# Top-k weights by halves, a later square root and fewer fillers in one expert layer, diagonal blocks on GpSimd in another

## The reference

```python
h = _rmsnorm(x, norm_w)
scores = jax.nn.softmax(flat @ router_w.T, axis=-1)
topk_w, topk_ids = lax.top_k(scores, K)                  # K = 4
topk_w = topk_w / jnp.sum(topk_w, axis=-1, keepdims=True)
act = jax.nn.silu(g) * u                                  # per chosen expert
routed = jnp.sum(y.reshape(T, K, H) * topk_w[..., None], axis=1)
shared = jax.nn.silu(flat @ sg) * (flat @ su) @ sd
out = residual + (routed + shared).reshape(B, S, H)
```

```python
scores = jax.nn.sigmoid((xf @ gate_w.T).astype(jnp.float32))
_, sel = jax.lax.top_k(scores + expert_bias, TOP_K)      # TOP_K = 2
xq = mxfp8_qdq(routed * ts_sorted[:, None])
h = jax.nn.silu(h1) * h3
routed_out = jax.lax.ragged_dot(mxfp8_qdq(h), w2q, counts)
```

## Time and profile before

| what | us |
|---|---|
| median of 3 runs | 1478.41 |
| lowest and highest | 1473.91, 1485.47 |
| the profiled execution | 1473.91 |
| its span | 1472.2 |
| mean granted clock of TensorE | 0.944 of full speed |

### The profile page before, as it was taken

How to read it: one execution, slowest core, us unless ns; L and a number is a source line. 1 busy time by engine, 2 the same in 40 slices (tenths; PEclk the granted TensorE clock), 3 DMA queues, 4 the chain that set the end, 5 groups by cost and what they waited for, 6 DMA issues and landing times. The chain is left out here.

```text
span 1472.2 us, 25588 instructions
## 1 busy us (share of the span) xinstructions
PE 1236.5 (84%) x9839; PEld 846.4 (57%) x9839; DVE 1145.4 (78%) x2253; ACT 872.1 (59%) x1155; POOL 296.9 (20%) x231
## 2 busy tenths in 40 slices
PE   3899998564887988877889999978896999998687
PEld 1577776442334555556656766745683766766454
DVE  5788786498888999929578999956896899897553
ACT  3677766522666787813166666734893667665453
POOL 0000000100141111000005155240460165155000
PEclk9999999877998999978999999999999999999889
DMA  6699989102005999983269998950554999989500
GB/s 240 118 182 178 198 164 177 57 1 90 11 1 105 185 200 196 192 188 66 97 109 196 184 186 166 167 148 22 173 172 135 167 171 173 173 153 167 108 1 8
DMA packets 561641, 199.55 MB, mean 136 GB/s; under 512 B 547200, under 2 KB 547584, under 8 KB 560256
## 3 DMA queue, kind: packets, MB, share of 16 engines
q1 hardware_dynamic: 561536, 198.15, 66.7%
HBM read 60.48 MB, written 0.26 MB: 41 GB/s over the span
## 5 line engine op out<-in xcount | busy, mean ns | idle before, releaser
L596 DVE SCALAR_TENSOR_TENSOR arena<-L_xattn_sm,L_xattn_rr,arena 128x1024 f16<-128x1024 f32 x192 | 274.9, 1472 | 11.2 <-ACT arena L495 10.9
L570 DVE CUSTOM_DVE_ANT_0 L_xattn_sm<-ps,L_xattn_bias 128x1024 f32<-128x1024 f32 x192 | 231.0, 1221 | 59.6 <-issue 56.6
L495 ACT ACTIVATE arena<-L_xattn_sm,L_xattn_rr 128x1024 f16<-128x1024 f32 x192 | 210.1, 1141 | 112.2 <-DVE L_xattn_rr L587 111.3
L399 PE MATMUL ps<-ctxT,L_xattn_qk 128*128 128x512 f16 x1152 | 267.1, 382 | 6.9 <-DVE L_xattn_qk L557 6.5
L485 ACT ACTIVATE L_xattn_sm<-L_xattn_sm,L_xattn_nm 128x2048 f32<-128x2048 f32 x96 | 192.2, 2002 | 77.0 <-DVE L_xattn_nm L579 76.1
L411 PE MATMUL ps<-arena,ctx 128*128 128x128 f16 x3072 | 194.9, 224 | 29.1 <-DMA arena<-arena 28.9
L411 PEld LDWEIGHTS ps<-arena,ctx 128*128 128x128 f16 x3072 | 182.7, 100 | 44.4 <-DMA arena<-arena 33.2
L399 PEld LDWEIGHTS ps<-ctxT,L_xattn_qk 128*128 128x128 f16 x1152 | 111.8, 99 | 135.9 <-DVE L_xattn_qk L557 9.0
L421 PEld LDWEIGHTS ps<-arena,ctx 128*128 128x128 f16 x1536 | 94.1, 98 | 22.8 <-DMA arena<-arena 5.4
L421 PE MATMUL ps<-arena,ctx 128*128 128x128 f16 x1536 | 102.2, 220 | 3.8 <-DMA arena<-arena 3.7
L2114 PE MATMUL ps<-arena 128*128 128x512 f16 x384 | 91.8, 391 | 0.0
(11 more groups left out here) (527 smaller groups left out, 2071.4 us busy)
## 6 DMA issues: line engine op xcount, KB each, us to landing
arena<-in_L_xattn_w SPq DMA_DIRECT2D x48, 320.0 KB, 4.3
L_ffn_ring<-in_L_ffn_experts SPq DMA_DIRECT2D x34, 384.0 KB, 3.6
arena<-in_L_ffn_experts SPq DMA_DIRECT2D x8, 768.0 KB, 8.7
arena<-arena SPq DMA_TRANSPOSE x199, 4.5
arena<-in_L_ffn_codes SPq DMA_DIRECT2D x1, 3072.0 KB, 12.1
arena<-in_L_ffn_scales SPq DMA_DIRECT2D x8, 384.0 KB, 22.9
arena<-in_L_attn_w SPq DMA_DIRECT2D x1, 2163.0 KB, 11.3
arena<-in_ctxT SPq DMA_DIRECT2D x1, 2048.0 KB, 7.6
```

The lines of the kernel that those rows point to most:

```text
L399: last = nc.tensor.matmul(ps[:, at, :], qk[:, h // 2, qp, h % 2, b * P:(b + 1) * P], k.ctxT[:, cp, b, at * 512:(at + 1) * 512], start=(a = ...
L495: nc.scalar.mul(pp[:, u % 2, 0, at], sm[:, u % 2, at], rr[:, u % 2:u % 2 + 1]).then_inc(s.p_high, 1)
L570: nc.vector.tensor_tensor_reduce(sm[:, u % 2, half * 1024:(half + 1) * 1024], ps[:, 2 * half:2 * half + 2, :].rearrange("p a n -> p (a n)" ...
L596: nc.vector.scalar_tensor_tensor(pp[:, u % 2, 1, at], sm[:, u % 2, at], rr[:, u % 2:u % 2 + 1], pp[:, u % 2, 0, at], ALU.mult, ALU.subtrac ...
```

## The change

In L2_ffn four things change. The top-k weights are made by a new function `top_weights`, for one token half at a time, with every instruction chained; both calls, with `activate(0)`, `activate(1)` and `activate(2)` around them, stand ahead of `w_low(3)`; `w_low(4)` comes in the loop. The factor 1/(QUP * ASC) is applied to all of `wt` at the end. ScalarE's Sqrt stands behind the weight splits of experts 0 and 1. The fillers at the start go from 22 to 13. In L3_ffn POOL makes the diagonal blocks, in four instructions of 8 x 128 columns, and ScalarE's 32 multiplications go.

```diff
+def top_weights(nc, dve, chain, choice, value, e, top, best, tmp, one, small, eps, out, b):
+
+    c, v = choice[:, b, :], value[:, b, :]
+    gt, eq, cum = tmp[:, 0, 0:e], tmp[:, 1, 0:e], tmp[:, 2, 0:e]
+    chain(nc.vector.max(best, c))
+    kth = best[:, top - 1:top]
+    chain(nc.vector.tensor_scalar(gt, c, kth, None, ALU.is_gt))
+    chain(nc.vector.tensor_scalar(eq, c, kth, None, ALU.is_equal))
+    chain(nc.vector.tensor_tensor_scan(cum, one[:, 0:e], eq, 0.0, ALU.mult, ALU.add))
+    chain(nc.vector.tensor_reduce(small[:, 0:1], gt, AX_X, ALU.add))
+
+    chain(nc.vector.tensor_scalar(small[:, 0:1], small[:, 0:1], -1.0, float(top), ALU.mult, ALU.add))
+    chain(nc.vector.scalar_tensor_tensor(eq, cum, small[:, 0:1], eq, ALU.is_le, ALU.mult))
+    chain(nc.vector.tensor_tensor(gt, gt, eq, ALU.add))
+    chain(nc.vector.tensor_tensor(gt, gt, v, ALU.mult))
+    chain(nc.vector.tensor_reduce(small[:, 1:2], gt, AX_X, ALU.add))
+    chain(nc.vector.tensor_scalar(small[:, 1:2], small[:, 1:2], eps, None, ALU.add))
+    chain(nc.vector.reciprocal(small[:, 1:2], small[:, 1:2]))
+    chain(nc.vector.tensor_scalar(out, gt, small[:, 1:2], None, ALU.mult))
...
-                keep_busy(k, 7, 22)
+                keep_busy(k, 7, 13)
...
                 ln_scalar(k, act, n)
-                w_high(0)
+                for e in range(2):
+                    w_high(e)
+                    w2_scale(e)
                 act.wait_ge(s.ms_ready, 1)
                 nc.scalar.activation(ms[:], ms[:], ACT.Sqrt, bias=k.zero[:]).then_inc(s.rms_ready, 1)
-                w2_scale(0)
-                for e in range(1, 3):
-                    w_high(e)
-                    w2_scale(e)
+                w_high(2)
+                w2_scale(2)
...
                 activate(0)
+                chain(nc.vector.memset(wt[:, :, ME:], 1.0))
+                for b in range(B):
+                    top_weights(nc, dve, chain, sc, sc, ME, MTOP, best[:], tmp, k.ones, small, 0.0,
+                                wt[:, b, 0:ME], b)
+                    activate(b + 1)
+                chain(nc.vector.tensor_scalar(wt[:], wt[:], 1.0 / (QUP * ASC), None, ALU.mult))
+                dve.wait_ge(s.x_started, 1)
                 w_low(3)
...
-                    if 2 <= e < MALL - 3:
+                    if 1 <= e < MALL - 3:
                         w_low(e + 3)
...
+            @block.gpsimd
+            def _(pool):
+                pool.wait_ge(s.m_ready, 1)
+                for j in range(2):
+                    for b in range(B):
+                        nc.gpsimd.tensor_tensor(
+                            dm[:, j, b, :, :], k.identb[:].rearrange("p (a t) -> p a t", a=1).broadcast_to([P, FE, P]),
+                            m[:, j, b, :].rearrange("p (e a) -> p e a", a=1).broadcast_to([P, FE, P]), ALU.mult)\
+                            .then_inc(s.diag_ready, 1)
...
-                act.wait_ge(s.m_ready, 1)
-                diagonals(0)
                 act.wait_ge(s.sgu_psum, 1)
...
-                diagonals(1)
```

More of the change, by code:

```diff
@@ L1643, in moe_layer @@
         mx = sb("mx", [P, B])
[L1644 to L1649, removed]
+        best = sb("best", [P, 8])
+        tmp = sb("tmp", [P, 3, ME])
+        small = sb("small", [P, 2])
         wt = sb("wt", [P, B, MALL])
@@ L1853, in _ @@
                 chain(last)
-                full = [P, B, ME]
-                def wide(v):
-                    return v.rearrange("p (b a) -> p b a", a=1).broadcast_to(full)
+                activate(0)
+                chain(nc.vector.memset(wt[:, :, ME:], 1.0))
                 for b in range(B):
[L1861 to L1866, removed]
-                w_low(3)
[L1868 to L1884, removed]
+                    top_weights(nc, dve, chain, sc, sc, ME, MTOP, best[:], tmp, k.ones, small, 0.0,
[3 more added lines that the diff above has]
+                dve.wait_ge(s.x_started, 1)
+                w_low(3)
                 for e in range(MALL):
```

## The result

| | before | after |
|---|---|---|
| median, 13 runs of each, us | 1482.41 | 1494.95 |
| lowest and highest | 1471.08, 1485.86 | 1486.83, 1499.56 |
| span of the profiled execution | 1472.2 | 1490.3 |
| mean granted clock of TensorE | 0.944 | 0.937 |

The ratio is 1.0095, with a 95% interval of 1.0075 to 1.0114: the changed kernel is slower by about 14 us (11 to 17). The two medians of the table lie 12.5 us apart, 0.85%, which is inside that interval. The forecast was 1492.3 us and 1.0094.

A forecast was written before the change was run, and what follows sets the result against it. TensorE was taken to bound L3_ffn's chain and L2_ffn's loop, with VectorE's order deciding ahead of the loop. L2_ffn's 6.6 us and L3_ffn's 7.3 sum to 13.9, on 1478.41 giving 1492.3 us (+0.94%), range 1482 to 1502.

The forecast's parts named there:

- Late Sqrt: L2_ffn, ScalarE: the Sqrt behind two weight splits comes 1.4 us later, with all on the path behind it; bounds 0.9 and 1.6.
- fewer fillers: L2_ffn, TensorE: 13 fillers leave 4.5 us idle, so the clock likely falls: +0.4 us, bounds 0 and 1.7.
- Top-k by halves: L2_ffn, VectorE: two chains of 13 instructions, 5.6 us, ahead of `w_low(3)` put TensorE's restart 2.8 us later (2.2 to 4.9).
- the four collisions: L2_ffn: four POOL instructions each hold up VectorE's top-k stretch by 0.45 us, 1.8 us in all.
- A whole round: L2_ffn: TensorE restarts with `up(3)` where it restarted with `up(4)`, costing one loop round, +1.96 us.
- Four turns of POOL: L3_ffn: four POOL instructions each hold VectorE 1.83 us ahead of `xq`: +6.1 us after overlap and slack; bounds 0 and 11.2.
- The slack: L3_ffn: `xq` is written 0.8 us before TensorE, released by its last filler, loads the first diagonal weight.
- TensorE's low clock behind the wait: L3_ffn: TensorE, idle until about 1434.6, starts the expert matmuls at the low level: +1.2 us (0 to 3).
- A: Rival, L3_ffn: POOL slips into VectorE's gaps or its cover is enough, no collision; 1485.0 us, chance 0.17.
- B: Rival, L3_ffn: POOL's instructions run at the slow rate, 3.24 us each; 1497.4 us, chance 0.18.
- C: Rival: the late L2_ffn restart is made up while the expert ring fills, no L3_ffn collision; 1476.1 us, chance 0.10.
- Its clause on the clock: Part of rival C: the shifts spare two low-clock starts of TensorE, 0.8 us and 1.5 us.

The follow-up runs named there:

- POOL's diagonals alone: Kernel before with only L3_ffn's diagonal blocks moved to POOL, four instructions ahead of `xq`: L2_ffn 84.15 us, L3_ffn 62.90 us, ratio 1.0043.
- POOL's second set: Kernel before with only the second set of diagonals on POOL, behind ScalarE's first set and the first `xq`: L2_ffn 85.17 us, L3_ffn 56.11, ratio 0.9982.
- the L2_ffn part alone: Changed kernel with L3_ffn as before: L2_ffn 90.98 us, L3_ffn 56.12 us, ratio 1.0025.
- two turns: Changed kernel with POOL's third and fourth diagonal instructions waiting for the first `xq`: L2_ffn 91.41 us, L3_ffn 58.15 us, ratio 1.0053.
- top-k alone: Kernel before with only the top-k weights by halves and `w_low(3)` behind them: L2_ffn 89.59 us, L3_ffn 52.59 us, ratio 1.0027.
- late Sqrt: Kernel before with only the Sqrt behind the splits of experts 0 and 1: L2_ffn 84.94 us, L3_ffn 56.11 us, ratio 1.0002.
- `w_low(4)` early: Kernel before with `w_low(4)` directly behind the running counts and `activate(2)` two instructions later: L2_ffn 83.94 us, L3_ffn 54.91 us, ratio 1.0011.
- `w_low` ahead: Changed kernel with `w_low(3)` ahead of the top-k weights and `w_low(4)` ahead of the scaling of `wt`: L2_ffn 88.82 us, L3_ffn 62.90, ratio 1.0073.
- 22 fillers: Changed kernel with 22 fillers again in L2_ffn: L2_ffn 91.24 us, L3_ffn 59.91 us, ratio 1.0088.

## Why the prediction was right, and where its terms were off

1. *Late Sqrt, +1.4, and fewer fillers, +0.4.* `activate(0)` came 13.66 us after the layer's start (1047.35 - 1033.69), against 12.54 before: +1.1 for both, not 1.8. Alone the Sqrt moved it by 0.9, as it did in the mean of six profiles against six. What was missed is that the edit also moves most of POOL's split off h, which gives back 0.3. The fillers' term should have been nothing (91.24 and 91.30 us): the matmuls at the low level had cover behind VectorE's `w_low(1)` and `w_low(2)`.
2. *Top-k by halves, +2.8.* From `activate(0)` to TensorE's restart 9.51 us (9.50 with the edit alone), 6.90 before: +2.6. The steps erred in opposite directions. Without collisions a half takes about 3.1 us, not 2.8 (its 13 instructions follow one another after 0.19 to 0.29); of the four collisions three came, 0.33 to 0.43 each.
3. *A whole round, +1.96.* It came: TensorE restarted with `up(3)` and had 31 up-projections to run from there, where it had 30; putting `w_low(3)` back took 2.5 us off. Above this, the restart took 2.74 us against 2.28, and with the next rounds +0.6. This the prediction had at nothing: it took both restarts to be at the low clock. But before, TensorE restarted at the full level (1046.62) and fell about 0.5 us later, while behind the long wait it started low (the last section has the row). Sum 1.1 + 2.6 + 2.0 + 0.6 = 6.3. That it lies so near 6.6 is in part luck: 0.9 too much in the first two items, 0.6 too little here.
4. *Four turns of POOL, +6.1.* The mechanism was right in its number of turns, in the instructions that pay and in what waits for them. Each POOL instruction took 1.87 us (7.46 for four) where I had 1.98 from the instruction of 768 columns, and VectorE lost 1.56 for each. Mask to `xq` therefore grew by 6.25, not 6.9. The slack was 0.5, not 0.8: even where TensorE waits for `xq`, in the kernel with POOL's diagonals alone, its first spread matmul starts 0.5 us behind the end of `xq`, and this I had counted as slack. TensorE's first expert matmul came 5.8 later in the kernel with that part alone (24.77 us into the layer against 19.01).
5. *TensorE's low clock behind the wait, +1.2.* In that kernel the first 32 matmuls took 8.08 us against 7.07, +1.0; together +6.8 of the 7.3. This pair can be trusted, since the clock at the head of the layer and under the second group of matmuls was alike: the four profiles with no turn ahead of `xq` and that same head took 56.11 or 56.12 us, and both with four turns 62.90. The profile of the changed kernel had another clock throughout. The mask came 0.73 us earlier, so that the first expert matmul came only 4.8 later; the first group of 32 took +0.6, the second 1.5 less than before (7.07 for 8.56), and the last fell to the low level and took +1.7 (5.17 us in the chain above, 3.51 before). That its sum is +5.35 is an accident of that profile. These parts are not the change's but the clock's, as the last section shows.

So of the sum of 13.9 us the pair of profiles shows 11.7, and with L3_ffn's 6.8 at a like clock 13.1. Over all profiles with one form of a layer against the other, L2_ffn went from a mean of 84.8 (before, POOL alone, POOL's second set) to 91.2 (after, the L2_ffn part alone, two turns) and L3_ffn from 55.2 (before, the L2_ffn part alone, top-k alone, late Sqrt, `w_low(4)` early) to 61.8 (after, POOL alone, `w_low` ahead, 22 fillers): 6.5 + 6.6 = 13.1 us, 0.88%. The ratio says 14.1 (0.0095 x 1482.4). The base moved: the kernel before measured 1482.41 in these runs, 4.0 over the three runs of the forecast, while the medians lie 12.5 apart for the 13.9 forecast. The two errors partly cancel, and so 1492.3 lies only 2.7 below the 1494.95 measured. The mechanism was right in both layers; that the time is met so closely is luck.

Of the rivals, A (no collision) fell with the stretched rows and with mask to `xq` at 5.53, 8.67 and 11.78 us for none, two and four turns. B (3.24 us for each) fell with 1.87. C (made up in the loop) fell with a loop that stayed at 1.96 us. Its clause on the clock, that the shifts would spare two starts at the low level, fell in L2_ffn: in the six profiles with the new top-k order the restart took 2.74 us each time. In L3_ffn the second group of 32 ran at full clock in two of the four profiles with four turns, but so it did in three of the seven with none.

## What to carry to other kernels

An idle engine is not a free one: POOL had nothing to do in this layer, but its multiplication with two SBUF inputs took VectorE's turn four times, and what counts is whether VectorE's instructions at that moment lie on the path. Four turns ahead of `xq` cost 6.25 us and two behind it nothing. Where one engine's list feeds a loop that runs without a gap, an operation moved behind a long chain costs its own delay and a whole round besides, if the loop's order then puts a step ahead of others that were ready.

## What the runs showed of the hardware that was not expected

First, unchanged code differs by several us between executions, and TensorE's clock takes part in it. Here is a stretch of the first 10 us of L3_ffn in the kernel before, by windows of 1 us (busy shares of the engines, then TensorE's granted clock):

```profile
1413.00:1414.00 1.00, 1.00 (x5) 0.30 (x4) 0.93 (x5) 1.00 (x1) 0.00 (x0) 1.00 0.00 0
...
1417.00:1418.00 1.00, 1.00 (x6) 0.82 (x4) 0.00 (x0) 0.98 (x2) 0.00 (x0) 0.50 0.00 0
```

And the same layer, the same code, in the kernel with top-k alone:

```profile
1431.00:1432.00 1.00, 0.88 (x9) 0.90 (x9) 0.00 (x0) 1.00 (x1) 0.00 (x0) 1.00 0.00 0
```

0.50 is 1.2 GHz, 1.00 is 2.4. In the kernel before the layer met the low level twice, here and again under its second group of expert matmuls; with top-k alone every window of the layer stood at 1.00. It took 56.11 us with the two, 52.59 without: 3.5 us, over half of what the change costs in it. What TensorE had done in this layer up to the first fall was the same in both. In the changed kernel the low level came in at about 5 us (0.61 in the first window below) and returned behind the wait:

```profile
1430.00:1431.00 1.00, 1.00 (x8) 1.00 (x7) 0.00 (x0) 1.00 (x1) 0.00 (x0) 0.61 0.00 0
...
1446.00:1447.00 1.00, 0.59 (x2) 0.21 (x3) 0.97 (x3) 0.42 (x1) 0.00 (x0) 1.00 0.00 0
1448.00:1449.00 1.00, 1.00 (x3) 0.21 (x2) 0.93 (x3) 1.00 (x4) 0.00 (x0) 0.50 0.00 0
```

It began its work behind the wait at the full level, against what I had said, and fell after that. In the three other profiles with four turns the forecast held: TensorE fell to the low level while it still waited and started there. With POOL's diagonals alone the first spread matmul was at 1438.72:

```profile
1436.00:1437.00 1.00, 0.00 (x0) 0.00 (x0) 0.93 (x3) 0.00 (x0) 0.00 (x0) 1.00 0.00 0
...
1438.00:1439.00 1.00, 0.28 (x1) 0.28 (x3) 0.97 (x3) 0.04 (x1) 0.00 (x0) 0.50 0.00 0
```

The same shows in L2_ffn. Behind the waits of 5.5 to 6.9 us ahead of `up(3)` all five profiles had TensorE start low (2.74 us for twelve matmuls). Behind 2.08 and 2.09 us, with the same code, one profile stayed at the full level (1.48 us) and the other, that of the kernel before, started at it and fell: the windows from 1046, 1047 and 1048 have 1.00, 0.57 and 0.50.

```profile
1046.00:1047.00 1.00, 0.38 (x4) 0.35 (x5) 1.00 (x3) 1.00 (x4) 0.52 (x1) 1.00 0.00 0
```

What decides between the courses was not tried, so it stays open, as does the share of the clock in the spread of the other layers.

Second, the price of a turn hardly depends on the size of VectorE's instruction: two-input ones on 2, 4 and 16 columns and a `tensor_scalar` on 2 paid 1.4 to 1.7 us each for a POOL instruction of 1.87, while the reduction and the reciprocal between them, in the same 7.46 us, paid nothing.
